# The experts' router: six powers per token, or one

## The chip, the cores and the metric

The kernel runs on one core of a Trainium2 chip. The metric is the device time of one execution in microseconds; lower is better.

## The reference

The input x has 4 sequences of 1024 tokens with 256 features, 4096 tokens in all. Two layers follow each other, each of a cross-attention to 77 context tokens and a feed-forward part. The feed-forward part of the first layer is a mixture of six experts, and the change lies in its router:

```
z = x @ proj_w.T                              # 6 numbers per token
q = tanh(z / 0.3)
logits = -(6 - q @ anchors.T) / 2 / clip(routing_temp, 0.1)
topk_logits, topk_idx = top_k(logits, 2)
topk_w = softmax(topk_logits)                 # two weights per token
expert_weights = onehot(topk_idx) . topk_w    # six, four of them zero
h = gelu(x @ w1[e])                           # for each of the six experts
x = x + sum_e (h[e] @ w2[e]) * expert_weights[e]
```

With two logits a >= b the softmax is 1 / (1 + e^(b-a)) and e^(b-a) / (1 + e^(b-a)).

## The kernel before

The 4096 tokens are cut into 8 blocks of 512 tokens (g = 0 to 7). The stages of the program follow one another: attention of layer 0 over 8 blocks, the experts over 8 blocks, attention of layer 1, and the last feed-forward part. Each engine has its own program, written out by hand in the order in which it is to run, and waits on counters ("semaphores") that other engines raise. Nothing is scheduled automatically.

In the experts' stage, each block g goes through its six experts e = 0 to 5. TensorE (PE) does in each step e: `hidden(g, e)` (six products of the tokens with w1, L135), then `output(g, e-2)` or, for e = 0 and 1, the outputs 4 and 5 of the block before (12 products with w2, L629). ScalarE (ACT) takes the gelu of `hidden` twice, once in full precision (`eh`, L516) and once rounded (`ehh`, L518). VectorE (DVE) or, for e = 3 and 5, GpSimd (POOL) forms the rest `ehl` = eh - ehh (`rest`, L587, and `rest_pooled`, L502). DVE then adds each expert's output to x with the weight of its expert (`add`, L597, four instructions, two for each of the two output banks). An output bank may be written again only when `add` of the expert before has read it.

The weights come out of the router. PE computes z early (`project`) and the dot products with the anchors (`compare`, L612) in step e = 0. DVE's `router(g)` stands in step e = 0 behind `add(g-1, 4)`: it forms the logits, counts for each expert how many stand above it (`erank`, 0 for the largest, 1 for the second), and takes logit minus largest logit (`ebelow`). POOL's `power(g)` raises e to that power (L508). DVE's `share(g)` stands in step e = 2 between `rest(g, 2)` and `add(g, 0)`: it keeps the two leading powers, sums them and divides.

DVE's order around it is: rest(g,0), add(g-1,4), router(g), rest(g,1), add(g-1,5), rest(g,2), share(g), add(g,0), add(g,1). PE's is: hidden(g,0), output(g-1,4), compare(g), hidden(g,1), output(g-1,5), hidden(g,2), output(g,0), a transpose of the next block's tokens (`turn`, L121), hidden(g,3), output(g,1). output(g,0) waits for add(g-1,5), and output(g,1) for add(g,0).

Between instructions of DVE that depend on one another the program puts a wait on the counter `erouter_chain`; `put` raises it. The names in the trace and in the listings below are those of the program with an e ahead of the experts' own: `eex` is `self.ex`, `egap` is `self.gap`.

Of the kernel before, what the change touches and what calls it, by code (L numbers as in the profile page):

```python
# [4 lines left out]
F32 = mybir.dt.float32  # L5
# [4 lines left out]
ALU = mybir.AluOpType  # L10
ACT = mybir.ActivationFunctionType
AX = mybir.AxisListType
# [4 lines left out]
P = 128  # L17
N = 512
NT = N // P
# [4 lines left out]
E, DE = 6, 128  # L24
# [15 lines left out]
def need(eng, sem, value):  # L40

    if value > 0:
        eng.wait_ge(sem, value)


class Places:


    def __init__(self, nc):
        self.nc = nc  # L50
# [376 lines left out]
class Experts:  # L427
# [5 lines left out]
    def __init__(self, nc, sem, place, norm, ps, m):  # L433
        self.nc, self.norm = nc, norm
        self.HID, self.OUT, self.RZ, self.RD = ps[2:4], ps[4:6], ps[6], ps[7]
        self.w1h, self.w1l = place.at("ew1h", m["ew1h"], [P, C, E * DE], F32R), place.at("ew1l", m["ew1l"], [P, C, E * DE], F32R)
        self.w2raw = place.at("ew2raw", m["ew2raw"], [P, E, D], F32)
        self.w2h, self.w2l = place.at("ew2h", m["ew2h"], [P, E, D], F32R), place.at("ew2l", m["ew2l"], [P, E, D], F32R)
        self.xh = [place.at(f"exh{k}", m[f"exh{k}"], [P, C, N], F32R) for k in range(2)]
        self.xl = [place.at(f"exl{k}", m[f"exl{k}"], [P, C, N], F32R) for k in range(2)]  # L440
        self.h = place.at("eh", m["eh"], [P, 2, N], F32)
        self.hh, self.hl = place.at("ehh", m["ehh"], [P, self.R, N], F32R), place.at("ehl", m["ehl"], [P, self.R, N], F32R)
        self.q = place.at("eq", m["eq"], [E, N], F32)
        at = [m["router"]]

        def small(name, shape, dt):
            size = 4
            for n in shape[1:]:
                size *= n
            at[0] += -(-size // 32) * 32  # L450
            return place.at("e" + name, at[0] - -(-size // 32) * 32, shape, dt)

        self.projf = small("projf", [P, C, E], F32)
        self.ph, self.pl = small("ph", [P, C, E], F32R), small("pl", [P, C, E], F32R)
        self.anchors = small("anchors", [E, E], F32)
        self.tempc, self.clip, self.half = small("tempc", [P, 1], F32), small("clip", [P, 1], F32), small("half", [P, 1], F32)
        self.euler = small("euler", [P, NT, E], F32)
        self.logit, self.above = small("logit", [P, NT, E], F32), small("above", [P, NT, E, E], F32)
        self.rank, self.top = small("rank", [P, NT, E], F32), small("top", [P, NT, 1], F32)
        self.below = small("below", [P, NT, E], F32)  # L460
        self.ex, self.exs = small("ex", [P, NT, E], F32), small("exs", [P, NT, E], F32)
        self.total, self.rtotal = small("total", [P, NT, 1], F32), small("rtotal", [P, NT, 1], F32)
        self.weight = small("weight", [P, 2, NT, E], F32)
        self.w1_in = sem("ew1_in")
        self.w2_in = sem("ew2_in")
        self.small_in = sem("esmall_in")
        self.cleared = sem("ecleared")
        self.w1h_ready = sem("ew1h_ready")
        self.w1_ready = sem("ew1_ready")
        self.w2h_ready = sem("ew2h_ready")  # L470
        self.w2_ready = sem("ew2_ready")
        self.router_chain = sem("erouter_chain")
        self.router_ready = sem("erouter_ready")
        self.z_done = sem("ez_done")
        self.q_ready = sem("eq_ready")
        self.dot_done = sem("edot_done")
        self.logit_ready = sem("elogit_ready")
        self.below_ready = sem("ebelow_ready")
        self.ex_ready = sem("eex_ready")
        self.weight_ready = sem("eweight_ready")  # L480
        self.hid_done = sem("ehid_done")
        self.h_ready = sem("eh_ready")
        self.hh_ready = sem("ehh_ready")
        self.hl_ready = [sem(f"ehl_ready{i}") for i in range(2)]
        self.out_done = sem("eout_done")
        self.added = sem("eadded")
        self.chain = 0
        self.OWNERS = [[e for e in range(E) if e not in self.POOLED], list(self.POOLED)]
# [16 lines left out]

    def power(self, pool, g):
        pool.wait_ge(self.below_ready, g + 1)
        self.nc.gpsimd.tensor_tensor(self.ex[:], self.euler[:], self.below[:], ALU.pow).then_inc(self.ex_ready, 1)  # L508
        pool.wait_ge(self.ex_ready, g + 1)


# [40 lines left out]
    def router(self, dve, g):  # L552
        nc = self.nc
        dve.wait_ge(self.dot_done, g + 1)
        nc.vector.tensor_scalar(self.logit[:], self.RD[:, 0:NT * E].rearrange("p (t e) -> p t e", e=E), 6.0, self.half[:, 0:1],
                                ALU.subtract, ALU.mult).then_inc(self.logit_ready, 1)
        dve.wait_ge(self.logit_ready, g + 1)
        for o in range(E):
            for lo, hi, op in ((0, o, ALU.is_gt), (o + 1, E, ALU.is_ge)):
                if lo < hi:  # L560
                    self.put(nc.vector.tensor_tensor(self.above[:, :, lo:hi, o], self.logit[:, :, o:o + 1].to_broadcast([P, NT, hi - lo]),
                                                     self.logit[:, :, lo:hi], op))
        self.put(nc.vector.reduce_max(self.top[:], self.logit[:], AX.X))
        dve.wait_ge(self.router_chain, self.chain)
        self.put(nc.vector.reduce_sum(self.rank[:], self.above[:], AX.X))
        need(dve, self.ex_ready, g)
        nc.vector.tensor_tensor(self.below[:], self.logit[:], self.top[:].to_broadcast([P, NT, E]),
                                ALU.subtract).then_inc(self.below_ready, 1)

    def share(self, dve, g):  # L570
        nc = self.nc
        dve.wait_ge(self.ex_ready, g + 1)
        dve.wait_ge(self.router_chain, self.chain)
        self.put(nc.vector.scalar_tensor_tensor(self.exs[:], self.rank[:], 2.0, self.ex[:], ALU.is_lt, ALU.mult))
        dve.wait_ge(self.router_chain, self.chain)
        self.put(nc.vector.reduce_sum(self.total[:], self.exs[:], AX.X))
        dve.wait_ge(self.router_chain, self.chain)
        self.put(nc.vector.reciprocal(self.rtotal[:], self.total[:]))
        dve.wait_ge(self.router_chain, self.chain)
        nc.vector.tensor_tensor(self.weight[:, g % 2, :, :], self.exs[:], self.rtotal[:].to_broadcast([P, NT, E]),  # L580
                                ALU.mult).then_inc(self.weight_ready, 1)
        dve.wait_ge(self.weight_ready, g + 1)
# [1087 lines left out]
```

## Time and profile before

| | us |
|---|---|
| median of 3 runs | 865.5 (864.38 to 866.55) |
| the profiled execution, its own time | 866.98 |
| its span, first to last instruction | 865.2 |
| experts' stage, first router to last output | about 254 to 443 |
| one of its blocks, from the first add to the first add of the next | 22.5 |

| engine | busy in the span |
|---|---|
| TensorE (PE) | 90% |
| VectorE (DVE) | 76% |
| ScalarE (ACT) | 60% |
| GpSimd (POOL) | 46% |

The profile is taken from one execution. Its spans of matmuls overlap, since they are pipelined; from the start of one to the start of the next is the time that PE spends on it. The times around one instruction, before and behind which its engine waits, say more here than the busy shares.

### The profile page before, as it was taken

Reading aid. Unit: us, or ns where it says so; the run is one execution under the profiler, and the core shown is the slowest. Engines: PE = TensorE matmul, PEld = TensorE weight load, DVE = VectorE, ACT = ScalarE, POOL = GpSimd, SP = SyncE. Lnnn points to the kernel's source line nnn. Section 1 sums busy time; section 2 is a strip of 40 time slices with the busy share of each in tenths; the row PEclk is TensorE's granted clock in tenths of the full one; section 3 lists DMA queues with packets and bytes.
Section 4 is the critical chain, followed back from the end, with each engine's and each line's share of the span. In section 5 each row is a group of like instructions: output and inputs, shape, how many; then the busy total and the mean of one; then the engine's idle time right before and its main releaser. Section 6 shows DMA issues by size and latency. Waiting matters only on the chain.

```text
span 865.2 us, 13721 instructions
## 1 busy us (share of the span) xinstructions
PE 774.8 (90%) x4452; PEld 568.9 (66%) x4452; DVE 659.9 (76%) x1576; ACT 520.1 (60%) x942; POOL 398.4 (46%) x323
## 2 busy tenths in 40 slices
PE   4799999999899999999988988988879999899996
PEld 3456556666467787777754544554458888788885
DVE  7657877777768777877777888888777778787784
ACT  3455565555554455544446675666668787788774
POOL 5523322223233433443311221222159998988995
PEclk9999999999999999999988999999999999999999
DMA  6965643355200000001075446555000000000001
GB/s 216 159 164 109 146 78 72 74 107 102 70 0 1 2 3 5 2 1 50 15 97 70 59 60 110 88 75 75 3 1 1 25 1 26 25 25 2 25 25 50
DMA packets 24817, 48.01 MB, mean 55 GB/s; under 512 B 3655, under 2 KB 6856, under 8 KB 24234
## 3 DMA queue, kind: packets, MB, share of 16 engines
q1 hardware_dynamic: 23224, 46.02, 27.8%
q10 hardware_dynamic: 1522, 1.11, 0.4%
q8 instruction: 37, 0.61, 0.3%
q14 instruction: 34, 0.28, 0.1%
HBM read 11.47 MB, written 4.19 MB: 18 GB/s over the span
## 4 chain that ended last, share of the span: by engine, by line
PE 52%; DVE 18%; POOL 11%; issue 7%; ACT 5%; DMA 5%; POOLq 0%; ACTq 0%; DVEq 0%
PE bank L135 15%; PE bank L396 5%; PE bank L371 5%; PE bank L629 5%; PE bank L421 5%; DMA qst<-mt 4%; PE bank L407 4%; DVE mx L327 4%; POOL eex L508 4%; PE bank L777 4%; POOL fy L696 3%; POOL frise L689 3%; PE bank L399 2%; PE bank L121 2%; DVE x L597 2%
## 5 line engine op out<-in xcount | busy, mean ns | idle before, releaser
L301 ACT ACTIVATE pt<-bank 77x512 f32<-77x512 f32 x256 | 146.4, 589 | 123.5 <-PE bank L399 76.4
L327 DVE TENSOR_REDUCE mx<-bank 128x4 f32<-128x308 f32 x256 | 108.9, 471 | 30.3 <-PE bank L374 17.8
L396 PE MATMUL bank<-qst,l_kst 128*77 128x512 f32 (+1 forms) x256 | 106.7, 431 | 19.3 <-DMA qst<-mt 13.3
L696 POOL TENSOR_TENSOR fy<-fpart,fg 128x512 f32<-128x512 f32 x64 | 103.9, 1624 | 9.4 <-DVE fpart L737 4.8
L371 PE MATMUL bank<-l_kblk,qh 128*128 128x308 f32 x256 | 89.7, 366 | 12.0 <-DVE mx L327 9.8
L689 POOL TENSOR_TENSOR frise<-fg,fg 128x512 f32<-128x512 f32 x64 | 90.1, 1408 | 9.0 <-POOL fy L696 4.7
L103 POOL TENSOR_TENSOR rstd<-var,minus_half 128x4 f32<-128x4 f32 x32 | 33.2, 1039 | 127.6 <-DVE var L98 74.9
L396 PEld LDWEIGHTS bank<-qst,l_kst 128*77 128x77 f32 (+1 forms) x256 | 36.8, 148 | 83.2 <-issue 48.8
L277 POOL TENSOR_TENSOR ol<-ot,oh 128x512 fp32r<-128x512 f32 x32 | 43.0, 1345 | 94.2 <-ACT oh L306 62.1
L371 PEld LDWEIGHTS bank<-l_kblk,qh 128*128 128x128 f32 x256 | 49.3, 193 | 55.9 <-issue 46.8
L737 DVE SCALAR_TENSOR_TENSOR fpart<-ffixed,frise 128x512 f32<-128x512 uint16 x64 | 58.6, 915 | 33.0 <-POOL frise L689 32.8
L597 DVE SCALAR_TENSOR_TENSOR x<-bank,eweight,x 128x256 f32<-128x256 f32 x192 | 79.5, 475 | 4.4 <-PE bank L629 4.1
L777 PE MATMUL bank<-fw2h,fyh 128*128 128x256 f32 x256 | 72.3, 282 | 3.5 <-DVE fyl L743 3.5
L407 PE MATMUL bank<-pt,l_vall 128*32 128x512 f32 x512 | 69.4, 614 | 6.4 <-DVE ut L335 3.8
L113 ACT ACTIVATE xn<-x,shift,rstd 128x256 f32<-128x256 f32 x128 | 68.1, 590 | 11.6 <-POOL shift L105 11.6
L777 PE MATMUL bank<-fw2l,fyh 128*128 128x256 f32 x256 | 71.9, 281 | 0.0
L777 PE MATMUL bank<-fw2h,fyl 128*128 128x256 f32 x256 | 71.8, 281 | 0.0
L706 ACT ACTIVATE fg<-ffixed 128x512 f32<-128x512 int16 x64 | 40.4, 632 | 45.4 <-DVE ffixed L731 45.2
L629 PE MATMUL bank<-ew2h,ehh 128*128 128x256 f32 x192 | 56.6, 295 | 10.3 <-DVE x L597 10.3
L629 PE MATMUL bank<-ew2l,ehh 128*128 128x256 f32 x192 | 54.7, 285 | 0.0
L629 PE MATMUL bank<-ew2h,ehl 128*128 128x256 f32 x192 | 54.5, 284 | 0.0
L731 DVE TENSOR_SCALAR ffixed<-bank 128x512 int32<-128x512 f32 x64 | 43.7, 683 | 12.0 <-PE bank L135 11.9
(179 smaller groups left out, 2144.2 us busy)
## 6 DMA issues: line engine op xcount, KB each, us to landing
qst<-qh SPq DMA_DIRECT2D x64, 256.0 KB, 6.7
qst<-ql SPq DMA_DIRECT2D x32, 256.0 KB, 9.0
out<-x SPq DMA_DIRECT2D x8, 512.0 KB, 2.6
qst<-ml SPq DMA_DIRECT2D x8, 480.0 KB
x<-in_x SPq DMA_DIRECT2D x3, 1024.0 KB, 12.7
weights<-in_mlp_w SPq DMA_DIRECT2D x2, 1024.0 KB, 5.1
mraw<-in_mask SPq DMA_DIRECT2D x8, 154.0 KB
x<-in_x SPq DMA_DIRECT2D x2, 512.0 KB, 5.5
```

The source lines that it names most:

```text
L113: last = self.nc.scalar.activation(self.xn[:, t:t + 1, :], self.tile(n, t), ACT.Identity, bias=self.shift[:, t, :], scale=self.rstd[:, t, :])
L135: last = self.nc.tensor.matmul(out, w, a, start=(first and k == 0), stop=(k == len(ops) - 1))
L301: self.nc.scalar.activation(self.pt[0:T, i // 4 % 2, i % 4, :], self.bank_of(G, i)[0:T, :], ACT.Exp).then_inc(self.probs, 1)
L327: self.nc.vector.reduce_max(out, banks[u % len(banks)][:, 0:4 * T].rearrange("q (p par t) -> q p par t", p=2, par=2), AX.X).then_inc(self. ...
L371: last = self.nc.tensor.matmul(bank, self.qh[:, c, tile], keys, start=True, stop=not layer.masked)
L396: last = self.nc.tensor.matmul(out, layer.kst[rows, layer.stack(c * HC + 2 * k + par), b * T:(b + 1) * T], self.qst[rows, self.slot(G), c ...
L407: last = self.nc.tensor.matmul(self.U[32 * k:32 * k + 32, :], layer.vall[:, self.batch(G), layer.value(c * HC + 2 * k + par), :], self.pt[ ...
L597: last = self.nc.vector.scalar_tensor_tensor(tile, part, self.weight[:, g % 2, 2 * k + t, e:e + 1], tile, ALU.mult, ALU.add)
L629: last = self.nc.tensor.matmul(self.OUT[k][:, t * D:(t + 1) * D], a[:, e % self.R, tile], w[:, e, :], start=(j == 0), stop=(j == 2))
L689: self.nc.gpsimd.tensor_tensor(self.rise[:, k % 2, :], self.g1[:, k % self.R, :], self.g0[:, k % self.R, :], ALU.subtract).then_inc(self.r ...
L696: self.nc.gpsimd.tensor_tensor(self.y[:, k % 2, :], self.part[:, k % 2, :], self.g0[:, k % self.R, :], ALU.add).then_inc(self.y_ready, 1)
L777: last = nc.tensor.matmul(self.OUT[2 * (g % 2) + t // 2][:, t % 2 * D:(t % 2 + 1) * D], a[:, k % self.R, t * P:(t + 1) * P], w[:, c, :], s ...
```

## The change

The power is now taken of one number per token. DVE's `router` masks `ebelow` with "rank is 1" (`esecond`), sums it over the six experts to get second logit minus first (`egap`), and POOL raises e to that: 4 elements per partition where there were 24 (the tile holds 4 tokens of each partition). In `share` the second weight is spread over the six experts again by the mask, 1 is put where the rank is 0, and the sum is simply 1 plus the power.

```
     def power(self, pool, g):
         pool.wait_ge(self.below_ready, g + 1)
-        self.nc.gpsimd.tensor_tensor(self.ex[:], self.euler[:], self.below[:], ALU.pow).then_inc(self.ex_ready, 1)
+        self.nc.gpsimd.tensor_tensor(self.ex[:], self.euler[:], self.gap[:], ALU.pow).then_inc(self.ex_ready, 1)
...
         self.put(nc.vector.reduce_sum(self.rank[:], self.above[:], AX.X))
+        self.put(nc.vector.tensor_tensor(self.below[:], self.logit[:], self.top[:].to_broadcast([P, NT, E]), ALU.subtract))
+        dve.wait_ge(self.router_chain, self.chain)
+        self.put(nc.vector.scalar_tensor_tensor(self.second[:], self.rank[:], 1.0, self.below[:], ALU.is_equal, ALU.mult))
+        dve.wait_ge(self.router_chain, self.chain)
         need(dve, self.ex_ready, g)
-        nc.vector.tensor_tensor(self.below[:], self.logit[:], self.top[:].to_broadcast([P, NT, E]),
-                                ALU.subtract).then_inc(self.below_ready, 1)
+        nc.vector.reduce_sum(self.gap[:], self.second[:], AX.X).then_inc(self.below_ready, 1)
 
     def share(self, dve, g):
         nc = self.nc
         dve.wait_ge(self.ex_ready, g + 1)
         dve.wait_ge(self.router_chain, self.chain)
-        self.put(nc.vector.scalar_tensor_tensor(self.exs[:], self.rank[:], 2.0, self.ex[:], ALU.is_lt, ALU.mult))
+        self.put(nc.vector.scalar_tensor_tensor(self.second[:], self.rank[:], 1.0, self.ex[:].to_broadcast([P, NT, E]), ALU.is_equal,
+                                                ALU.mult))
+        self.put(nc.vector.tensor_scalar(self.total[:], self.ex[:], 1.0, None, ALU.add))
         dve.wait_ge(self.router_chain, self.chain)
-        self.put(nc.vector.reduce_sum(self.total[:], self.exs[:], AX.X))
-        dve.wait_ge(self.router_chain, self.chain)
+        self.put(nc.vector.scalar_tensor_tensor(self.exs[:], self.rank[:], 0.0, self.second[:], ALU.is_equal, ALU.add))
         self.put(nc.vector.reciprocal(self.rtotal[:], self.total[:]))
         dve.wait_ge(self.router_chain, self.chain)
         nc.vector.tensor_tensor(self.weight[:, g % 2, :, :], self.exs[:], self.rtotal[:].to_broadcast([P, NT, E]),
```

`euler` (the tile that holds e) and `ex` shrink to 4 elements per partition, and `gap` and `second` are new. PE's and ACT's instructions stay as they were, and so do POOL's but for the size of the power.

The end of `router` on DVE in block g, and the two instructions behind it, before:

```order
L563 TENSOR_REDUCE etop<-elogit 128x4
L565 TENSOR_REDUCE erank<-eabove 128x24 [waits erouter_chain]
L567 TENSOR_TENSOR ebelow<-elogit,etop 128x24 [waits eex_ready]
L587 TENSOR_TENSOR ehl<-eh,ehh 128x512 [waits eout_done,ehh_ready]
L597 SCALAR_TENSOR_TENSOR x<-bank,eweight,x 128x256 [waits eadded,eout_done]
```

The same place with the change (the lines of the file are shifted by up to 5):

```order
L564 TENSOR_REDUCE etop<-elogit 128x4
L566 TENSOR_REDUCE erank<-eabove 128x24 [waits erouter_chain]
L567 TENSOR_TENSOR ebelow<-elogit,etop 128x24
L569 SCALAR_TENSOR_TENSOR esecond<-erank,ebelow 128x24 [waits erouter_chain]
L572 TENSOR_REDUCE egap<-esecond 128x4 [waits eex_ready,erouter_chain]
L592 TENSOR_TENSOR ehl<-eh,ehh 128x512 [waits eout_done,ehh_ready]
L602 SCALAR_TENSOR_TENSOR x<-bank,eweight,x 128x256 [waits eadded,eout_done]
```

Two instructions, each with a wait for the one before, stand ahead of the signal to POOL and ahead of rest(g,1) and add(g-1,5).

`share` on DVE, between rest(g,2) and add(g,0), before:

```order
L587 TENSOR_TENSOR ehl<-eh,ehh 128x512 [waits eout_done,ehh_ready]
L574 SCALAR_TENSOR_TENSOR eexs<-erank,eex 128x24 [waits erouter_chain,eex_ready]
L576 TENSOR_REDUCE etotal<-eexs 128x4 [waits erouter_chain]
L578 RECIPROCAL ertotal<-etotal 128x4 [waits erouter_chain]
L580 TENSOR_TENSOR eweight<-eexs,ertotal 128x24 [waits erouter_chain]
```

And with the change:

```order
L592 TENSOR_TENSOR ehl<-eh,ehh 128x512 [waits eout_done,ehh_ready]
L578 SCALAR_TENSOR_TENSOR esecond<-erank,eex 128x24 [waits erouter_chain,eex_ready]
L580 TENSOR_SCALAR etotal<-eex 128x4
L582 SCALAR_TENSOR_TENSOR eexs<-erank,esecond 128x24 [waits erouter_chain]
L583 RECIPROCAL ertotal<-etotal 128x4
L585 TENSOR_TENSOR eweight<-eexs,ertotal 128x24 [waits erouter_chain]
```

Four instructions became five, and of the five two have no wait: three steps, each waiting for the one before, where there were four.

## Rows read from the trace of the kernel before

**Rows 1.** The page: the span, and the chain that ended last by line.

```profile
span 865.2 us, 13721 instructions
...
PE bank L135 15%; PE bank L396 5%; PE bank L371 5%; PE bank L629 5%; PE bank L421 5%; DMA qst<-mt 4%; PE bank L407 4%; DVE mx L327 4%; POOL eex L508 4%; PE bank L777 4%; POOL fy L696 3%; POOL frise L689 3%; PE bank L399 2%; PE bank L121 2%; DVE x L597 2%
```

**Rows 2.** The power's line L508 and what waited (durations ns min/median/max).

```profile
L508 POOL TENSOR_TENSOR eex<-eeuler,ebelow x8: 4162/4698/4704, 255.6 to 413.3; 128x24 f32<-128x24 f32 x8
...
  DVE eexs L574: 6.9, 6
```

**Rows 3.** DVE in block 5: start us, us, instruction, idle before and its releaser.

```profile
367.94 0.17 DVE L567 TENSOR_TENSOR ebelow<-elogit,etop 128x24 f32<-128x24 f32 x1
368.24 0.69 DVE L587 TENSOR_TENSOR ehl<-eh,ehh 128x512 fp32r<-128x512 f32 x1
368.85 1.65 DVE L597 SCALAR_TENSOR_TENSOR x<-bank,eweight,x 128x256 f32<-128x256 f32 x4
371.05 0.69 DVE L587 TENSOR_TENSOR ehl<-eh,ehh 128x512 fp32r<-128x512 f32 x1 [0.56 <-ACT ehh L518]
372.98 0.18 DVE L574 SCALAR_TENSOR_TENSOR eexs<-erank,eex 128x24 f32<-128x24 f32 x1 [1.24 <-POOL eex L508]
...
373.84 1.66 DVE L597 SCALAR_TENSOR_TENSOR x<-bank,eweight,x 128x256 f32<-128x256 f32 x4
```

**Rows 4.** POOL and ACT in block 5, same columns.

```profile
368.26 4.69 POOL L508 TENSOR_TENSOR eex<-eeuler,ebelow 128x24 f32<-128x24 f32 x1 [1.89 <-DVE ebelow L567]
...
367.61 0.59 ACT L518 ACTIVATE ehh<-bank 128x512 fp32r<-128x512 f32 x1
```

**Rows 5.** PE in block 5: ends of hidden, starts of output.

```profile
369.51 0.39 PE L135 MATMUL bank<-exl,ew1h 128*128 128x512 f32 x1
369.86 0.36 PE L629 MATMUL bank<-ew2h,ehh 128*128 128x256 f32 x1
...
372.73 0.39 PE L135 MATMUL bank<-exh,ew1l 128*128 128x512 f32 x1
372.95 0.40 PE L135 MATMUL bank<-exl,ew1h 128*128 128x512 f32 x1
374.87 0.36 PE L629 MATMUL bank<-ew2h,ehh 128*128 128x256 f32 x1 [1.52 <-DVE x L597]
```

**Rows 6.** The power of 4 elements, line L103 (columns as rows 2).

```profile
L103 POOL TENSOR_TENSOR rstd<-var,minus_half x32: 1006/1010/1531, 8.1 to 790.2; 128x4 f32<-128x4 f32 x32
```

**Rows 7.** DVE: two short instructions without a wait between them.

```profile
385.71 0.17 DVE L97 TENSOR_SCALAR minus_mean<-mv 128x4 f32<-128x4 f32 x1
385.79 0.17 DVE L98 TENSOR_SCALAR var<-mv 128x4 f32<-128x4 f32 x1
```

**Rows 8.** DVE and PE in block 4, with the shorter power.

```profile
349.07 0.69 DVE L587 TENSOR_TENSOR ehl<-eh,ehh 128x512 fp32r<-128x512 f32 x1
350.46 0.18 DVE L574 SCALAR_TENSOR_TENSOR eexs<-erank,eex 128x24 f32<-128x24 f32 x1 [0.70 <-POOL eex L508]
...
351.43 0.40 PE L135 MATMUL bank<-exl,ew1h 128*128 128x512 f32 x1
352.34 0.35 PE L629 MATMUL bank<-ew2h,ehh 128*128 128x256 f32 x1 [0.51 <-DVE x L597]
```

**Rows 9.** DVE in blocks 0 and 2, where L574 did not wait.

```profile
259.24 0.69 DVE L587 TENSOR_TENSOR ehl<-eh,ehh 128x512 fp32r<-128x512 f32 x1
260.07 0.18 DVE L574 SCALAR_TENSOR_TENSOR eexs<-erank,eex 128x24 f32<-128x24 f32 x1
...
305.36 0.69 DVE L587 TENSOR_TENSOR ehl<-eh,ehh 128x512 fp32r<-128x512 f32 x1 [2.74 <-ACT ehh L518]
```

**Rows 10.** Chain of waits behind the stage, and granted clock (PEclk) by stretch.

```profile
430.57 1.43 PE bank L629 x12
...
440.12 2.66 PE bank L629 x12
...
439.00:442.00 3.00, 2.90 (x13) 2.43 (x14) 1.98 (x6) 0.59 (x1) 0.00 (x0) 0.50 1.07 131
```

More of the change, by code:

```diff
@@ L456, in __init__ @@
         self.tempc, self.clip, self.half = small("tempc", [P, 1], F32), small("clip", [P, 1], F32), small("half", [P, 1], F32)
-        self.euler = small("euler", [P, NT, E], F32)
+        self.euler = small("euler", [P, NT, 1], F32)
         self.logit, self.above = small("logit", [P, NT, E], F32), small("above", [P, NT, E, E], F32)
@@ L460, in __init__ @@
         self.below = small("below", [P, NT, E], F32)
-        self.ex, self.exs = small("ex", [P, NT, E], F32), small("exs", [P, NT, E], F32)
+        self.gap, self.ex = small("gap", [P, NT, 1], F32), small("ex", [P, NT, 1], F32)
+        self.exs, self.second = small("exs", [P, NT, E], F32), small("second", [P, NT, E], F32)
         self.total, self.rtotal = small("total", [P, NT, 1], F32), small("rtotal", [P, NT, 1], F32)
```

## The prediction

> **What bounds the kernel now.** I read the page first. The chain that ended last is PE's for the most part, but it puts 4% of the span on POOL's power L508 [rows 1]: a small operation that stood in the path again and again. The second view is that line itself. Its 8 instructions take 4.70 us at the median, and DVE's first instruction of `share` waited for it 6 times, 6.9 us in all [rows 2]. So the power costs much and DVE waits little for it, since it runs beside `rest` and `add`. 8 x 4.70 = 37.6 us is not what can be won; to see what can, one block has to be laid out engine by engine.
>
> I take block 5. Blocks 1, 3, 6 and 7 read alike, with the same wait of 1.23 or 1.24 us at L574; together with block 4's 0.70 these are the 6.9 us. DVE signals `ebelow` at 368.11 (367.94 + 0.17) [rows 3], POOL computes from 368.26 to 372.95 [rows 4], and `share` starts at 372.98. DVE had begun rest(5,2) at 371.05. The step from the start of such a `rest` to the next instruction that waits for nothing is 0.61 us (368.24 to 368.85), so DVE could have begun `share` at 371.66: it stands 1.32 us late for POOL alone. `share` then runs to 373.84, 0.86 us in four steps of 0.215, and output(5,1) on PE starts at 374.87, 1.03 us behind the start of add(5,0) [rows 3, 5].
>
> On PE, a product L135 takes 0.22 to 0.23 us from start to start (372.73 to 372.95) [rows 5]; I take 0.23, so PE was done with hidden(5,3) at 372.95 + 0.23 = 373.18 and stood idle for 1.69 us until output(5,1). This is the most that a faster `share` can return in a block. It is a gap of the bounding engine; what stands behind it in the block (output, turn, hidden, the gelus, the next router) hangs on it in a row, so what is won at this place moves all that follows.
>
> **The change part by part.**
>
> *The power itself.* POOL already raises 4 elements per partition to a power in `invert` (L103): 1.01 us at the median over 32 [rows 6]. The same operation, with the same two tiles in SBUF and the same shape, so I take 1.01 us for the new L508. The operand's values differ: the eight powers of before lie between 4.16 and 4.70 us [rows 2], so values can matter by some 12%. Bounds: 1.0 us, and if the 24-element row scaled with nothing, 4.7 us; the second is a rival below.
>
> *Two more instructions before the signal.* `esecond` waits for `ebelow` and `egap` for `esecond`. A dependent short instruction of DVE costs 0.215 us, as the steps of `share` do. The signal moves from 368.11 to about 368.55. With the same 0.15 us to POOL's start, the power runs from 368.70 to 369.71. DVE asks for it at 371.66, so there are 1.95 us of room: the power, up to a length of 2.96 us, is hidden by rest(5,1), add(4,5) and rest(5,2). If that cover were gone, every further us of it would be paid.
>
> *What stands behind the two on DVE.* rest(5,1) and add(4,5) are queued behind them, and PE's output(5,0) waits for the first half of that add. rest(5,1) started at 368.24 not because DVE was late but because ACT's `ehh` ended at 367.61 + 0.59 = 368.20 [rows 4]. Two instructions without a wait between them start 0.08 us apart (385.71 and 385.79) [rows 7], so DVE alone could have begun it at 368.02; there is 0.22 of slack. The two instructions cost 0.43, so `rest` moves to 368.45, add(4,5) by the same 0.21, and output(5,0) from 369.86 to 370.07, since PE was there already at 369.51 + 0.23 = 369.74 [rows 5]. That pushes hidden(5,3) too: PE is free at 373.18 + 0.21 = 373.39. Bounds of this term: nothing, if `ebelow` no longer waits where it did, and 0.43 if there is no slack. rest(5,2) doesn't move: it waited 0.56 us for ACT [rows 3], more than 0.21.
>
> *`share`.* Five instructions in three dependent steps. With 0.08 us between two that don't wait [rows 7], a step with a pair costs 0.08 + 0.215 = 0.295, and the whole 2 x 0.295 + 0.215 = 0.80 us instead of 0.86. Reading 4 elements spread over 24 should cost what `ertotal` spread over 24 does in the last step already, so nothing is added for it. add(5,0) starts at 371.66 + 0.80 = 372.46, and PE may start output(5,1) at 372.46 + 1.03 = 373.49.
>
> The Trainium skill speaks against this term. "VectorE: DVE Perf Modes", section "The DRAIN you can't avoid", says that a Vector instruction is followed by an emptying of the pipe, that leaving out the semaphores between instructions saves nothing, and (section "Rules for kernel authors") that their number is to be kept small. By that page five instructions would take 5 x 0.215 = 1.08 us, and `share` would grow. The row at 385.79 says otherwise for instructions this short; I go by the rows, and the other outcome is a rival.
>
> *Sum of a block.* output(5,1) starts at the later of 373.49 (DVE) and 373.39 (PE): 373.49, which is 374.87 - 373.49 = 1.38 us earlier. Both engines arrive within 0.1 us of each other, so nearly all of PE's gap is gone, and a still faster `share` would give nothing more here. For blocks 1, 3, 5, 6 and 7: 5 x 1.38 = 6.9 us.
>
> *Block 4.* `share` could have started at 349.07 + 0.61 = 349.68 instead of 350.46: with its 0.06, output(4,1) would go from 352.34 to 351.50, but PE is free only at 351.43 + 0.23 = 351.66 [rows 8]. Gain 0.68. *Block 0.* `share` could start at 259.24 + 0.61 = 259.85 instead of 260.07 [rows 9]: 0.22 + 0.06 = 0.28. *Block 2.* DVE waited 2.74 us for ACT ahead of rest(2,2) at 305.36 [rows 9], so only the 0.06 of `share`.
>
> *Sum.* 6.9 + 0.68 + 0.28 + 0.06 = 7.9 us. The profiled execution took 866.98 us (span 865.2 and 1.8 around it), so its like should take 859.1; the median of the runs shown is 865.5, 1.5 below the profiled one, and gives 865.5 - 7.9 = 857.6.
>
> *What is hit next.* Nothing in the stage hangs on the clock on the wall: its loads were done before. Behind it PE's granted clock falls. In 439 to 442 it was 0.50, that is 1.2 GHz, after DVE's maxima had kept PE waiting, and there one output of twelve products took 2.66 us instead of 1.43 [rows 10]. When the stage ends 8 us earlier, such a fall may come at other work, or once more or less: about 1.2 us either way, which I put into the range and not into the sum.
>
> **The rivals.** What can be told from no change in this kernel is about 0.3%, 2.6 us.
>
> 1. *The forecast*, about 857.6 us (855.5 to 859). Chance 0.80.
>
> 2. *The unwaited instructions cost full steps.* `share` 1.08 us: output(5,1) at 371.66 + 1.08 + 1.03 = 373.77, gain 1.10, five times 5.5; block 4 gains 0.78 - 0.22 = 0.56, block 0 nothing, block 2 loses 0.22. Together 5.8, so 859.7. The Trainium skill's rule above is this one. For it speaks that no row has a 24-element scalar_tensor_tensor in front of an unwaited one; against it [rows 7]. Chance 0.10.
>
> 3. *The gain is given back.* The attention stage behind starts earlier, and PE's clock falls at more places. To bring the result within 0.3%, 5.3 of the 7.9 us must go, more than four more falls like that of rows 10 at 1.2 us each. The clock depends on what PE did just before, and that stays the same in kind. About 863.5. Chance 0.06, with what I have overlooked on the path.
>
> 4. *Slower: the power's length hangs on something other than the number of elements.* It stays at 4.70 us, or near it, because of the values or of a fixed part. Place: POOL L508 to DVE L574. It starts 0.44 us later, and `share` returns 0.06: +0.38 us in seven blocks (0, 1 and 3 to 7), -0.06 in block 2, where it would still end in time: +2.6 us, 868.1. It decides from a length of 4.70 - 0.38 = 4.32 us on; below 2.96 it costs nothing. Against it stand 32 rows of the same operation at 1.01 us [rows 6]. Chance 0.02.
>
> There is a remainder of 0.02 on the fast side: PE's whole gap of 1.69 us falls away in five blocks because the first product behind an unwaited start is also shorter, 5 x 0.31 = 1.5 us more, 856.1.
>
> **How the numbers follow.** The time is that of the first case. Its own bounds: with no slack for the two instructions output(5,1) hangs on PE at 373.61, gain 1.26 and sum 7.3; with the whole gap 9.4. The range adds the 1.2 us of the clock to either side of 856.1 and 859.7 and is cut a little at the ends, 855.0 to 861.0; it holds cases 1 and 2 and the fast remainder. Faster by over 0.3% are cases 1 and 2 and the fast remainder, 0.92; within 0.3% case 3, 0.06; slower case 4, 0.02.
>
> **What the new profile would show.** L508 at 128x4 and 1.0 us, ending some 2 us before DVE asks for it; no idle time before the first instruction of `share` (L578) that POOL ended; `share` 0.80 us from L578 to the add (1.08 would be rival 2); rest(g,1) 0.2 us later against the start of `router`; PE's gap before output(g,1) about 0.1 us instead of 1.69; the blocks 21.1 us apart instead of 22.5. If the blocks do stand 1.4 us closer and the time doesn't fall by 6 us or more, the loss is behind 430 us in the old trace's count, and the rows of the clock there would show it. The prediction is wrong from the root if L508 still takes over 3 us, or if some engine that I took to follow (ACT's gelus, POOL's rests) turns out to be the next one to wait for within the block.

## The result and the profile after

The changed kernel takes 856.95 us (median of 4 runs, 855.17 to 857.45); beside it the kernel before took 866.02 (864.38 to 866.58). The ratio is 0.9896, with a 95% interval of 0.9881 to 0.9911: 9.1 us faster. A second set of runs gave 855.23 against 865.89, ratio 0.9878 (0.9853 to 0.9903).

The page of the changed kernel: span, busy times, and the chain that ended last by line.

```profile
span 854.8 us, 13752 instructions
PE 772.9 (90%) x4452; PEld 568.5 (67%) x4452; DVE 661.6 (77%) x1600; ACT 519.7 (61%) x942; POOL 372.5 (44%) x323
...
PE bank L135 15%; PE bank L634 6%; PE bank L396 5%; PE bank L371 5%; PE bank L421 5%; DMA qst<-mt 4%; PE bank L407 4%; DVE mx L327 4%; POOL fy L701 4%; PE bank L782 3%; POOL frise L694 3%; PE bank L399 2%; PE bank L121 2%; DVE x L602 2%; DVE fpart L742 2%
```

The router's power, 4% of the chain in [rows 1], has left the list. POOL's busy time fell by 26 us; the kernel gained a third of that, since most of it ran beside other work.

DVE around the router of block 5 in the changed kernel, which answers to [rows 3] (start us, us, instruction, idle before and its releaser):

```profile
364.17 0.18 DVE L567 TENSOR_TENSOR ebelow<-elogit,etop 128x24 f32<-128x24 f32 x1
364.38 0.18 DVE L569 SCALAR_TENSOR_TENSOR esecond<-erank,ebelow 128x24 f32<-128x24 f32 x1
364.60 0.18 DVE L572 TENSOR_REDUCE egap<-esecond 128x4 f32<-128x24 f32 x1
364.69 0.68 DVE L592 TENSOR_TENSOR ehl<-eh,ehh 128x512 fp32r<-128x512 f32 x1
365.29 1.65 DVE L602 SCALAR_TENSOR_TENSOR x<-bank,eweight,x 128x256 f32<-128x256 f32 x4
367.30 0.69 DVE L592 TENSOR_TENSOR ehl<-eh,ehh 128x512 fp32r<-128x512 f32 x1 [0.35 <-ACT ehh L519]
367.91 0.17 DVE L578 SCALAR_TENSOR_TENSOR esecond<-erank,eex 128x24 f32<-128x24 f32 x1
368.00 0.16 DVE L580 TENSOR_SCALAR etotal<-eex 128x4 f32<-128x4 f32 x1
368.19 0.18 DVE L582 SCALAR_TENSOR_TENSOR eexs<-erank,esecond 128x24 f32<-128x24 f32 x1
368.30 0.17 DVE L583 RECIPROCAL ertotal<-etotal 128x4 f32<-128x4 f32 x1
368.50 0.18 DVE L585 TENSOR_TENSOR eweight<-eexs,ertotal 128x24 f32<-128x24 f32 x1
368.72 1.66 DVE L602 SCALAR_TENSOR_TENSOR x<-bank,eweight,x 128x256 f32<-128x256 f32 x4
```

The reader is to see three things. L578 no longer has a wait for POOL. It starts 0.61 us behind rest(5,2), which waits for ACT alone. And from L578 to the add there are 0.81 us, with 0.09 to 0.11 between the two of a pair and about 0.2 where there is a wait. POOL and PE at the same place (answering to [rows 4, 5]; the power ends at 366.24, 1.67 us before DVE asks for it):

```profile
364.92 1.32 POOL L509 TENSOR_TENSOR eex<-eeuler,egap 128x4 f32<-128x4 f32 x1 [2.32 <-DVE egap L572]
```

```profile
366.31 0.36 PE L634 MATMUL bank<-ew2h,ehh 128*128 128x256 f32 x1 [0.17 <-DVE x L602]
...
369.41 0.40 PE L135 MATMUL bank<-exl,ew1h 128*128 128x512 f32 x1
369.74 0.36 PE L634 MATMUL bank<-ew2h,ehh 128*128 128x256 f32 x1
369.94 0.28 PE L634 MATMUL bank<-ew2l,ehh 128*128 128x256 f32 x1
```

PE is free at 369.41 + 0.23 = 369.64 and starts output(5,1) at 369.74: a gap of 0.10 us where there were 1.69.

The stage as a whole, from the first logit to the first maximum of the attention behind it, in windows of the kernel before and of the changed one (length, then busy us of each engine and granted clock):

```profile
253.72:432.19 178.47, 168.14 (x1057) 142.48 (x1058) 139.89 (x467) 86.61 (x164) 72.40 (x46) 1.00 0.03 9
```

```profile
253.80:424.34 170.54, 167.74 (x1057) 142.57 (x1058) 141.54 (x490) 86.53 (x164) 46.36 (x46) 1.00 0.03 9
```

178.47 - 170.54 = 7.93 us won in the stage. The window ends with the first maximum, and the last outputs of the experts come behind it, between the attention's first pieces [rows 10]; below, "the stage" is this window. The spans differ by 10.4; the other 2.5 us lie behind it: 2.0 in the attention, where the granted clock was not the same (experiment 1), and 0.56 in the last feed-forward part, for which no cause is shown.

### The profile page after: what moved, and what is told of

Same layout as the page of the kernel before. It is cut to its first block, busy times and chain, and to the rows that moved or that the text cites. A ratio compares the mean times of both kernels' runs of the same rounds, so it can differ in the third digit from the quotient of the medians.

```text
span 854.8 us, 13752 instructions
## 1 busy us (share of the span) xinstructions
PE 772.9 (90%) x4452; PEld 568.5 (67%) x4452; DVE 661.6 (77%) x1600; ACT 519.7 (61%) x942; POOL 372.5 (44%) x323
## 4 chain that ended last, share of the span: by engine, by line
PE 53%; DVE 19%; issue 8%; POOL 8%; ACT 6%; DMA 5%; POOLq 0%; ACTq 0%; DVEq 0%
PE bank L135 15%; PE bank L634 6%; PE bank L396 5%; PE bank L371 5%; PE bank L421 5%; DMA qst<-mt 4%; PE bank L407 4%; DVE mx L327 4%; POOL fy L701 4%; PE bank L782 3%; POOL frise L694 3%; PE bank L399 2%; PE bank L121 2%; DVE x L602 2%; DVE fpart L742 2%
## 5 line engine op out<-in xcount | busy, mean ns | idle before, releaser
L103 POOL TENSOR_TENSOR rstd<-var,minus_half 128x4 f32<-128x4 f32 x32 | 33.2, 1037 | 125.3 <-DVE var L98 72.2
L503 POOL TENSOR_TENSOR ehl<-eh,ehh 128x512 fp32r<-128x512 f32 x16 | 20.7, 1294 | 81.2 <-ACT ehh L519 81.2
```

## The experiments

The whole time of one kernel varies by some us between executions, and experiment 1 looks at where. The length of the stage, from the first logit to the first maximum (windows as above), doesn't: I judge by it, and give the medians beside it.

| kernel | stage us | against changed | profiled run's time | median of runs |
|---|---|---|---|---|
| before | 178.47 | +7.93 | 866.98 | 866.02 |
| before, again | 178.50 | +7.96 | 863.77 | one run |
| changed | 170.54 | | 856.55 | 856.95 |
| changed, again | 170.57 | +0.03 | 855.32 | 855.23 |
| old size of power | 180.52 | +9.98 | 869.85 | 865.97 |
| two powers | 170.54 | 0.00 | 860.77 | 856.67 |
| three powers | 173.02 | +2.48 | 864.56 | 863.09 |
| share with all waits | 172.50 | +1.96 | 858.65 | 860.34 |
| short power only | 170.83 | +0.29 | 853.34 | 857.60 |
| share first | 169.09 | -1.45 | 859.02 | 857.67 |
| short router | 170.57 | +0.03 | 854.02 | one run |
| both | 168.06 | -2.48 | 854.70 | 854.52 |
| both, again | 168.03 | -2.51 | 853.99 | 854.05 |
| spaced rest | 173.19 | +2.65 | 856.93 | one run |

**1. Both kernels again.** Is the 2.5 us behind the stage the change's?

> The kernel before the change once more, for a second profile. The changed kernel's profile is 7.9 us ahead at the end of the experts' stage and 10.4 at the end of the program; between, PE's granted clock was 1.00 in stretches where before it was 0.81 to 0.87. Theory (the falls of the clock behind the stage lie differently from one execution to the next): in this profile the experts' stage takes the same time within 0.1 us as in the first profile of the kernel before, but the first 40 us behind it differ by 0.5 to 2 us. Rival (the falls belong to the kernel before, and the change avoids them): the same falls at the same places.

> The changed kernel again, beside the next one. The stage should read 170.5 us again within 0.1, and the stretch from the first maximum of the next attention to the first row of the last feed-forward part, 190.45 us in the first profile of the changed kernel and 192.5 and 191.5 in two of the kernel before, should again differ from execution to execution with the granted clock. Median 856 to 858.

The stage read 178.50 and 170.57, within 0.1 us of the first profiles as expected. The median of the changed kernel, 855.23, lies below the 856 to 858 that I expected. The stretch from the first maximum to the first row of the last feed-forward part (`ffixed`) took 192.47 and 191.53 us in the kernel before and 190.45 and 189.59 in the changed one; in the other variants, which differ in the stage before only, 189.67 to 195.87. So it moves by 6 us, and more than I had written; `two powers`, whose stage is that of the changed kernel to the hundredth, took 194.67 where the changed one took 190.45. The granted clock goes with it. In the first 40 us behind the first maximum (the third number from the end is the clock), the kernel before, the same again, the changed one, and `two powers`:

```profile
432.19:472.19 40.00, 33.17 (x142) 19.37 (x140) 30.36 (x81) 20.70 (x37) 4.72 (x9) 0.83 0.61 80
```

```profile
429.93:469.93 40.00, 33.23 (x144) 19.12 (x143) 30.82 (x81) 20.82 (x38) 4.71 (x9) 0.87 0.62 82
```

```profile
424.34:464.34 40.00, 33.04 (x149) 19.42 (x147) 31.84 (x84) 22.30 (x41) 4.71 (x9) 0.91 0.66 87
```

```profile
424.38:464.38 40.00, 33.48 (x137) 19.80 (x139) 30.15 (x80) 20.60 (x37) 4.57 (x9) 0.83 0.59 75
```

The changed kernel again read 0.91. The 33rd instruction of the attention's maxima came 40.80 and 40.29 us behind the first in the kernel before (they differ by 0.5, the low end of what I expected), 38.66 and 38.38 in the changed one, and 41.42 in `two powers`. That the clock differs between two executions of one kernel (0.83 and 0.87) is shown, and that stretches at the lower level take longer is in [rows 10]. Whether the changed kernel has fewer such stretches on average stays open: its two profiles had the higher clock, and `two powers` did not.

**2. Is it the power's length?** The change keeps its new DVE code but gets the old number of elements.

```
+        self.ex = self.wide[:, :, 0:1]
...
-        self.nc.gpsimd.tensor_tensor(self.ex[:], self.euler[:], self.gap[:], ALU.pow).then_inc(self.ex_ready, 1)
+        self.nc.gpsimd.tensor_tensor(self.wide[:], self.euler[:], self.gap[:].to_broadcast([P, NT, E]), ALU.pow).then_inc(self.ex_ready, 1)
```

> The changed kernel, but POOL raises e to the gap spread over all six experts, 24 elements per partition; DVE reads one of the six, so the result is the same. Theory (only the power's length counts, and the two more instructions of DVE are a cost that it must first earn back): the power is 4.2 to 4.7 us again, DVE waits for it in seven blocks, and each is 0.38 us later than before the change: 868 to 869 us, some 11 to 12 above the changed kernel. Rival (most of the gain came from share's new form or from the clock behind the stage): at least 3 us below the kernel before, 863 or less.

The powers took 4.46 or 4.47 us and once 4.71, and DVE waited for them seven times, 9.4 us in all. The two lines of the waits that name them (us in total, times, longest):

```profile
POOL ewide L510 <- DVE egap L573: 23.3, 8, 3.7
DVE esecond L579 <- POOL ewide L510: 9.4, 7, 1.7
```

The stage is 9.98 us longer than in the changed kernel and 2.05 longer than before, where seven times 0.38 less 0.06 had been expected, 2.6. From logit to logit, block 0 was 0.38 longer than before; blocks 1, 3, 5, 6 and 7 only 0.14 to 0.18, since their powers took 4.47 us and not 4.70; and block 4 was 0.89 longer, since on top of the later signal its power took 4.71 and not 4.16 (why, the last section says). The median, 865.97 over 10 runs from 863.04 to 871.4 (ratio 1.0006, 0.9984 to 1.0028), lies 2 to 3 us below what I expected. Without the shorter power the change wins nothing.

**3. How much room?** One or two unused powers in front of the real one; with one:

```
+        self.nc.gpsimd.tensor_tensor(self.spare[:, 0, :, :], self.euler[:], self.gap[:], ALU.pow)
         self.nc.gpsimd.tensor_tensor(self.ex[:], self.euler[:], self.gap[:], ALU.pow).then_inc(self.ex_ready, 1)
```

> The changed kernel with a second, unused power of 4 elements in front of the real one. In the changed kernel's profile DVE asks for the power 3.13 us after its signal and POOL starts 0.14 us behind the signal, so there are 2.99 us of room; two powers take about 2.65 us. Theory (the power is hidden by what lies between router and share): no change, 857 us within 1. Rival (any length of the power is on the path, since it stands in the chain of waits): 1.3 us in each of 7 blocks, 866.

> Two unused powers in front of the real one, about 3.95 us in all, 0.96 us beyond the room of 2.99. Theory: DVE waits about 0.96 us for POOL in blocks 1, 3, 5, 6 and 7 and similar in 4, so 5 to 6 us more than the changed kernel: 862 to 863. If the powers overlap on POOL when no wait lies between them, less. Rival (any length counts): 2.6 us in each of 7 blocks, 875.

POOL in block 5 with two powers and, below, with three; and DVE's start of `share` with three:

```profile
364.94 1.32 POOL L510 TENSOR_TENSOR espare<-eeuler,egap 128x4 f32<-128x4 f32 x1 [2.32 <-DVE egap L574]
366.23 1.00 POOL L511 TENSOR_TENSOR eex<-eeuler,egap 128x4 f32<-128x4 f32 x1
```

```profile
366.41 1.32 POOL L510 TENSOR_TENSOR espare<-eeuler,egap 128x4 f32<-128x4 f32 x1 [2.32 <-DVE egap L575]
367.70 1.00 POOL L511 TENSOR_TENSOR espare<-eeuler,egap 128x4 f32<-128x4 f32 x1
368.68 1.00 POOL L512 TENSOR_TENSOR eex<-eeuler,egap 128x4 f32<-128x4 f32 x1
...
369.72 0.18 DVE L581 SCALAR_TENSOR_TENSOR esecond<-erank,eex 128x24 f32<-128x24 f32 x1 [0.24 <-POOL eex L512]
```

Two powers end 2.29 us behind the start of the first and cost nothing: 170.54 us, the same stage to the hundredth. Three end 3.27 us behind it, just past the room of 2.99, and the stage grows by 2.48, with 2.1 us of waits in six blocks: five blocks are 0.31 longer, and block 4, where the third power took 1.43 us, is 0.93 longer. Less than the 5 to 6 expected, because I had taken 1.32 us for each and the second and third took 1.00. The end of the room lies between 2.3 and 3.3 us, as computed. The median of 863.09 shows more than the stage's 2.5. The ten runs fall into two groups: four with a mean granted clock of 0.983 to 0.985 took 857.05 to 858.1 us, six with 0.974 to 0.978 took 862.88 to 864.56. So the rest goes with the clock; why six of these ten had the lower one isn't shown.

**4. Does `share` still count?** Each pair gets a wait between its two.

```
+        dve.wait_ge(self.router_chain, self.chain)
         self.put(nc.vector.tensor_scalar(self.total[:], self.ex[:], 1.0, None, ALU.add))
...
+        dve.wait_ge(self.router_chain, self.chain)
         self.put(nc.vector.reciprocal(self.rtotal[:], self.total[:]))
```

> The changed kernel with a wait between the two instructions of each pair in share, so that its five instructions are five dependent steps of 0.215 us: 1.08 instead of 0.80 us. Theory (DVE, not PE, is the later of the two at output(g,1)): 0.27 us more in each of 7 to 8 blocks, 2 us in all, 859. Rival (PE's own work is the bound there, share has room): no change, 857.

+1.96 us in the stage, as expected, and the median of 860.34 is 1.3 above the expected 859; `share` now runs 1.07 us, from the first to the last of these rows of DVE:

```profile
368.37 0.18 DVE L578 SCALAR_TENSOR_TENSOR esecond<-erank,eex 128x24 f32<-128x24 f32 x1
368.58 0.17 DVE L581 TENSOR_SCALAR etotal<-eex 128x4 f32<-128x4 f32 x1
...
369.44 0.88 DVE L604 SCALAR_TENSOR_TENSOR x<-bank,eweight,x 128x256 f32<-128x256 f32 x2
```

This is what rival 2 would have cost. Left without waits the two start 0.09 us apart, with one 0.21, so the rule of the Trainium skill on the pipe's emptying ("VectorE: DVE Perf Modes", section "The DRAIN you can't avoid"), that leaving out semaphores saves nothing, doesn't describe these instructions of 4 and 24 elements. The same section says that a next instruction which isn't held starts earlier; my prediction left that out, and these rows agree with it.

**5. One part alone.** The kernel before, with the power taken of 4 of its 24 elements; the other 20 are a constant 1, so the weights are not the reference's and this kernel is for the time alone.

```
-        self.nc.gpsimd.tensor_tensor(self.ex[:], self.euler[:], self.below[:], ALU.pow).then_inc(self.ex_ready, 1)
+        self.nc.gpsimd.tensor_tensor(self.ex[:, :, 0:1], self.euler[:, :, 0:1], self.below[:, :, 0:1], ALU.pow).then_inc(self.ex_ready, 1)
...
+                        nc.gpsimd.memset(ex.ex[:], 1.0)
```

> The kernel before with one part of the change: the power is taken of 4 elements per partition, and router and share stay as they were; the other 20 elements are a constant, so the weights are not those of the reference. Theory (all of the gain is POOL's length up to the room): share 0.86 us and nothing pushed behind the router: 5 x 1.32 + 0.68 + 0.22 = 7.5 us in the stage against 7.9 for the whole change, so 857 to 858. Rival (the three steps of share and the shorter sum carry a good part): 860 or more.

178.47 - 170.83 = 7.64 us against 7.93 for the whole change: the extra DVE work and the three steps of `share` nearly pay for each other.

**6. What bounds the block now?** `share` ahead of rest(g,2); a router without the counts; and both. The short router:

```
top = reduce_max(logit);  first = (logit is_equal top);  others = first * -1024 + logit
sec = reduce_max(others); gap = sec - top;               rank = (others is_equal sec)
```

Each step but the last waits for the one before, and `share` uses the two masks as they are. Its result is that of the reference unless two logits of a token are equal.

> The changed kernel with share(g) ahead of rest(g,2) on DVE. The power is ready 1.7 us before, so share need not wait for ACT's ehh(g,2). Theory (share behind rest(g,2) starts 0.35 us after DVE is free, since rest waits for ACT): output(g,1) can start when PE is free, 0.1 us earlier per block, 0.5 to 1 us in all, 856.3; no more, since PE is then the bound. Rival (rest(g,2) is late for somebody): slower, 858 or more.

> The short router alone, with share behind rest(g,2) as in the changed kernel. Theory (output(g,1) hangs on DVE through ACT's ehh(g,2), rest(g,2) and share, and only by 0.1 us less on PE): 0.9 us less work in the router give nothing at output(g,1), and the stage from the first logit to the first maximum stays at 170.5 us within 0.3. Rival (the router's length is on the path by itself): 0.2 us or more per block, 169 us or less.

> share ahead of rest(g,2), and a router without the counts: largest logit, mask of it, largest of the others, gap, mask of the second. Some 0.9 us less work on DVE ahead of rest(g,1) and add(g-1,5); two equal largest logits in a token would come out otherwise than in the reference. Theory: rest(g,1) waits for ACT again, output(g,0) on PE is no longer pushed by 0.21 us and output(g,1) starts when PE is free: 0.3 us per block, 2 to 2.5 us in all, 854.6. Rival (PE bound by its own work already): within 0.5 us of the changed kernel.

> The short router with share ahead of rest(g,2) again, on the same chip as the changed kernel. The stage read 168.06 us against 170.54, so 2.5 us less in the median, if the clock behind the stage treats both alike: 854 to 855.5.

The short router alone gives nothing (170.57), though from the logit to the end of `egap` or of the last mask it takes DVE 0.74 us less (1.39 instead of 2.13, where I had expected 0.9): rest(5,2) waits 0.56 us for ACT again. `share` first gives 1.45, more than the 0.5 to 1 expected, and both together 2.48 and 2.51. DVE in block 5 of `short router`:

```profile
362.82 1.65 DVE L600 SCALAR_TENSOR_TENSOR x<-bank,eweight,x 128x256 f32<-128x256 f32 x4
365.03 0.69 DVE L590 TENSOR_TENSOR ehl<-eh,ehh 128x512 fp32r<-128x512 f32 x1 [0.56 <-ACT ehh L521]
365.63 0.18 DVE L577 TENSOR_TENSOR esecond<-erank,eex 128x24 f32<-128x24 f32 x1
```

and PE of `share first`, the last product of hidden(5,3) and the first of output(5,1):

```profile
368.11 0.40 PE L135 MATMUL bank<-exl,ew1h 128*128 128x512 f32 x1
368.34 0.28 PE L634 MATMUL bank<-ew2h,ehh 128*128 128x256 f32 x1
368.46 0.28 PE L634 MATMUL bank<-ew2l,ehh 128*128 128x256 f32 x1
```

Here PE goes on without a gap. The expectation had counted the 0.10 us of PE's gap and forgotten that the first step behind a waited start is 0.20 us instead of 0.12 (369.74 to 369.94 in the changed kernel, 368.34 to 368.46 here): about 0.18 us together, 0.2 by the distance of the blocks' logits (21.17 and 20.97). Five such blocks make 0.9. The rest, 0.58 us, comes from block 2, which the expectation had left out: there rest(2,2) waits 2.53 us for ACT in the changed kernel, `share` now runs during that wait, and the block takes 22.75 us instead of 23.33. With the gap gone, PE is the bound and the router's length reaches it through add(g-1,5) and output(g,0): that is why the short router is worth nothing alone and 1.0 us on top, 0.2 in each of five blocks. The median of `share` first, 857.67, missed the 856.3 that I expected and isn't below the changed kernel's; its gain is shown in the stage alone. The medians (854.52 and 854.05; ratios to before 0.9891, 0.9862 to 0.9919, and 0.9874, 0.9846 to 0.9901) are the lowest of the medians; beside the second of them, the changed kernel had 855.23 (0.9853 to 0.9903), and the intervals overlap. That `both` beats the changed kernel is shown for the stage, by 2.5 us twice, and not for the whole time.

**7. Why 1.32 us?** Three short spare instructions behind `egap`, so that rest(g,1) starts behind the power and not ahead of it.

> The changed kernel with three short spare instructions on DVE behind egap, so that rest(g,1) starts some 0.4 us behind the start of POOL's power instead of 0.2 us ahead of it. In the profiles so far the length of a power goes with that distance: 1.32 and 1.55 us where rest started 0.23 ahead or just with it, 1.01 where it started later or not at all, with the same operands. Theory (a power that starts while DVE reads the two inputs of rest is held until DVE has read them): 1.01 us for all powers but those with another such rest under way. Rival (the operands' values, or DVE being busy in general): still 1.32. In the stage, rest and add are 0.64 us later and PE becomes the later of the two at output(g,1): 0.54 us more per block, 3 us in all.

All eight powers took 1.01 us (the first and the last, POOL), and in block 5 `rest` began 0.38 us behind the power's start:

```profile
253.80 1.01 POOL L510 TENSOR_TENSOR eex<-eeuler,egap 128x4 f32<-128x4 f32 x1 [2.12 <-DVE egap L573]
...
407.14 1.01 POOL L510 TENSOR_TENSOR eex<-eeuler,egap 128x4 f32<-128x4 f32 x1 [3.70 <-DVE egap L573]
```

```profile
364.32 0.69 DVE L599 TENSOR_TENSOR ehl<-eh,ehh 128x512 fp32r<-128x512 f32 x1
```

The same operands in the same kernel gave 1.32 us without the spare instructions, so the values are not what makes the difference. The stage grew by 2.65 us, where 3 were expected: PE waits 0.79 us for output(5,0) instead of 0.17 and then goes on without a gap at output(5,1).

## Why the prediction was right

It said 857.6 us, and 856.95 was measured. The mechanism held, and so did its size in the stage; that the two times lie 0.65 us apart is partly luck. The kernel before read 866.02 beside the changed one, 0.5 above the 865.5 that I counted from, and the median fell by 9.1 where the stage gave 7.9. Step by step:

- *What can be won is what DVE waits for at `share`, and PE's gap behind it.* Right. The waits of 6.9 us and the gap of 1.69 us became 0 and 0.10; the stage gave 7.93 us against the sum of 7.9. Two small errors offset each other in it: the five blocks gave 6.8 instead of 6.9, and block 4 gave 0.79 instead of 0.68. Experiment 2 shows that the power's length is the cause, experiment 3 where it stops to count.
- *The power, 1.01 us.* Mis-sized: 1.32, and 1.55 in block 4. It cost nothing, since the room was computed at 1.95 us beyond it. The reason that I gave for the spread of the old ones, the operands' values, was wrong (experiment 7 and the section below).
- *Two more instructions before the signal, 0.43 us, of which 0.21 reach `rest`.* Right: counted from the start of `ebelow`, `rest` starts 0.52 us behind (364.17 to 364.69) where it had been 0.30 (368.24 - 367.94): 0.22. rest(5,2) still waited for ACT, 0.35 us, that is 0.56 less 0.21.
- *`share`, 0.80 us.* Measured 0.81. Experiment 4 shows the other outcome and its price, 1.96 us. What I said of the page of the Trainium skill was half of its section (experiment 4).
- *Both engines arrive within 0.1 us at output(g,1).* Right, DVE the later by 0.10, as computed. Experiment 6 confirms it from both sides: a shorter router alone gives nothing, and `share` first takes away the 0.10.
- *Blocks.* 21.17 us from logit to logit (362.65 to 383.82) against 22.51: 1.34 instead of 1.38, and 1.36 to 1.38 in the other four. In block 4 output(4,1) starts 0.69 us earlier against the logit, as computed, without a wait; the first step behind it is then shorter by 0.08, which I had put only into the fast remainder.
- *What is hit next.* The clock behind the stage moved as feared, and I put 1.2 us either way where executions with the same instructions in that stretch differ by more: from 189.6 to 195.9 us over all the variants. Here it fell out in favour, so that the span of the profile fell by 10.4; whether the 1.2 us by which the median fell beyond 7.9 are of this kind too isn't shown.

## What to carry to other kernels

The cost of a small operation in the path is read from who waits for it and for how long, not from its own duration: 37.6 us of power hid all but 6.9 us of waits, and the gain of the stage could be summed from the gap of the bounding engine, less what the new work pushes. When the gap is closed, look at the order of independent pieces on the engine that follows; here `share` ahead of `rest` gave 1.4 us more in the stage, and a shorter router gave something only after that. Where the whole time scatters with the clock, compare the length of the stage.

## What the runs showed of the hardware that I had not expected

A power on POOL that starts while DVE runs a `rest` (128x512, two inputs from SBUF) takes longer, by up to 0.54 us. With the same operation, shape and operands: 1.32 us where `rest` had begun 0.23 us before, 1.55 where it began with it (block 4 of the changed kernel, 343.70 and 343.71), and 1.01 or 1.00 where it began later or was over, as the second power in experiment 3. Block 4 of the changed kernel, DVE and POOL:

```profile
343.70 0.69 DVE L592 TENSOR_TENSOR ehl<-eh,ehh 128x512 fp32r<-128x512 f32 x1
```

```profile
343.71 1.55 POOL L509 TENSOR_TENSOR eex<-eeuler,egap 128x4 f32<-128x4 f32 x1 [3.70 <-DVE egap L572]
```

The old powers show the same steps: 4.16 us in block 4, where `rest` came 0.43 later, 4.48 in block 0, where it had begun 0.23 before, 4.70 in the others, where it began 0.02 before [rows 3, 4]; the excess is 0.32 and 0.54 in both kernels. Blocks 0 and 4 of the kernel before, DVE and POOL:

```profile
255.33 0.68 DVE L587 TENSOR_TENSOR ehl<-eh,ehh 128x512 fp32r<-128x512 f32 x1
```

```profile
255.56 4.48 POOL L508 TENSOR_TENSOR eex<-eeuler,ebelow 128x24 f32<-128x24 f32 x1 [1.69 <-DVE ebelow L567]
```

```profile
346.69 0.69 DVE L587 TENSOR_TENSOR ehl<-eh,ehh 128x512 fp32r<-128x512 f32 x1 [0.57 <-ACT ehh L518]
```

```profile
346.26 4.16 POOL L508 TENSOR_TENSOR eex<-eeuler,ebelow 128x24 f32<-128x24 f32 x1 [3.26 <-DVE ebelow L567]
```

So a power that starts within such a `rest` ends as if it had begun 0.54 us behind the start of `rest`: 1.55 us behind it for 4 elements and 4.71 for 24, whether the power starts with it or 0.23 later. That it is held until DVE has read its inputs is my reading of this; no row shows the reading itself. `rest` took 0.68 or 0.69 either way, and a `rest` that starts after the power, as in experiment 7 and in block 4 above, lengthens neither. An `add` doesn't do it, with one of its two large inputs in PSUM (`bank`): the second power of experiment 3 starts at 366.23, during add(4,5), and takes 1.00. DVE there:

```profile
365.31 1.65 DVE L604 SCALAR_TENSOR_TENSOR x<-bank,eweight,x 128x256 f32<-128x256 f32 x4
```

The Trainium skill names a shared interface for this ("GPSIMD Engine Reference", section "1. Specifications": POOL shares its way to SBUF with VectorE, with contention where a DVE instruction has two SBUF inputs). The trace agrees, and adds the size and that, here, only a power that starts behind the start of `rest` is held.

By the two unheld lengths, a power costs (4.16 - 1.01) / 20 = 0.16 us for each element of a partition and some 0.4 us besides; this is an estimate from two sizes alone.
